# Macaron block on one core: expert rows stored raw with their mean and root, and a new order of the work ahead of the second router

## The reference

```python
x = x + 0.5 * ffn(layernorm(x))
x = x + mamba(layernorm(x))
x = x + 0.5 * ffn(layernorm(x))
```

## Time and profile before

| | us |
|---|---|
| median of 3 runs | 460.59 (459.33 to 460.80) |
| profiled execution | 461.21 |
| its span | 459.4 |
| TensorE busy | 404.0 (88%) |
| VectorE busy | 307.4 (67%) |
| ScalarE busy | 240.0 (52%) |
| GpSimd busy | 277.8 (60%) |

### The profile page before, as it was taken

How to read it: one execution, slowest core, us unless ns; L and a number is a source line. 1 busy time by engine, 2 the same in 40 slices (tenths; PEclk the granted TensorE clock), 3 DMA queues, 4 the chain that set the end, 5 groups by cost and what they waited for, 6 DMA issues and landing times.

```text
span 459.4 us, 9998 instructions
## 1 busy us (share of the span) xinstructions
PE 404.0 (88%) x2636; PEld 316.4 (69%) x2637; DVE 307.4 (67%) x761; ACT 240.0 (52%) x575; POOL 277.8 (60%) x262
## 2 busy tenths in 40 slices
PE   8779999999995998989979889984799999999940
PEld 6359999999994343434335346671499999999930
DVE  4824555555554967999989999999455555555516
ACT  4535444444434656686765867434454444444404
POOL 2167777777433252688685787765377777776330
PEclk9769999999997799999979999987699999999985
DMA  7942111112103200000000000001111111112026
GB/s 262 374 158 82 49 50 45 45 44 44 31 21 93 93 0 0 2 0 1 0 0 0 0 1 0 1 1 53 57 53 44 47 44 51 45 44 37 22 55 227
DMA packets 11964, 25.03 MB, mean 54 GB/s; under 512 B 3485, under 2 KB 4260, under 8 KB 11936
## 3 DMA queue, kind: packets, MB, share of 16 engines
q1 hardware_dynamic: 6944, 15.38, 9.5%
q0 software_dynamic: 4992, 9.32, 7.4%
HBM read 17.34 MB, written 8.26 MB: 56 GB/s over the span
## 4 chain that ended last, share of the span: by engine, by line
PE 65%; DVE 13%; ACT 7%; DMA 5%; issue 4%; POOL 4%; SPq 0%; POOLq 0%; ACTq 0%; DVEq 0%
PE ps L835 30%; PE ps L860 15%; PE ps L970 7%; DVE ring_space L1344 3%; DMA ring_space<-expert_rows 2%; ACT shared L705 2%; DVE stats L1097 2%; PE ps L830 2%; ACT ps L697 2%; POOL shared L486 2%; PE ps L957 2%; PE ps L951 2%; PE ps L903 1%; DMA xg<-xn_rows,get_i 1%; POOL rstd L398 1%
## 5 line engine op out<-in xcount | busy, mean ns | idle before, releaser
L835 PE MATMUL ps<-xT,w_now 128*128 128x128 f32 x1248 | 154.1, 277 | 0.8 <-ACT xT L574 0.7
L835 PEld LDWEIGHTS ps<-xT,w_now 128*128 128x128 f32 x1248 | 147.3, 194 | 1.4 <-ACT xT L574 1.1
L1226 DVE TENSOR_TENSOR hidden<-ps,hidden 128x256 f32<-128x256 f32 x156 | 58.9, 419 | 94.6 <-PE ps L835 94.6
L591 ACT ACTIVATE hidden<-ps 128x256 f32<-128x256 f32 x156 | 51.4, 381 | 111.2 <-PE ps L835 111.1
L434 POOL DMA_INDIRECT expert_rows<-ysb,put_i x78 | 79.9, 1024 | 46.5 <-DVE ysb L1234 30.1
L426 POOL DMA_INDIRECT xg<-xn_rows,get_i x78 | 80.6, 1034 | 45.1 <-issue 21.2
L486 POOL TENSOR_TENSOR shared<-ring_space,shared 128x512 f32<-128x512 f32 x64 | 81.9, 1287 | 35.5 <-DVE ring_space L1344 29.6
L860 PE MATMUL ps<-w_down,hidden 128*128 x624 | 82.1, 275 | 0.0
L970 PE MATMUL ps<-shared,consts 128*128 128x512 f32 x128 | 71.7, 644 | 7.6 <-POOL shared L486 7.4
L860 PEld LDWEIGHTS ps<-w_down,hidden 128*128 128x128 f32 x624 | 75.7, 192 | 0.2
L705 ACT COPY shared<-ps 128x512 f32<-128x512 f32 x64 | 37.6, 587 | 35.5 <-DVE ring_space L1344 18.2
(11 more groups left out here) (161 smaller groups left out, 410.6 us busy)
## 6 DMA issues: line engine op xcount, KB each, us to landing
w_gate_up<-in_experts SPq DMA_DIRECT2D x8, 512.0 KB, 8.6
xn_rows<-xn SPq DMA_DIRECT2D x8, 256.0 KB, 4.0
w_down<-in_experts SPq DMA_DIRECT2D x1, 2048.0 KB, 11.9
ring_space<-expert_rows SPq DMA_DIRECT2D x4, 512.0 KB, 5.9
xg<-xn_rows,get_i POOLq DMA_INDIRECT x78, 2.6
expert_rows<-ysb,put_i POOLq DMA_INDIRECT x78, 2.3
x<-in_x_rows SPq DMA_DIRECT2D x4, 256.0 KB, 4.5
ring_space<-expert_rows SPq DMA_DIRECT2D x4, 256.0 KB, 3.5
```

The lines of the kernel that those rows point to most:

```text
L591: nc.scalar.activation(gelu[:, slot % 2, half], ps[:, GATE_BANK[slot % 2], half], ACT.Gelu).then_inc(gelu_done, 1)
L835: m = pe.matmul(ps[:, bank, f * P:(f + 1) * P], w_now[:, slot % W_SLOTS, first + f * P:first + (f + 1) * P], xT[:, slot % X_SLOTS, :], sta ...
L1226: dve.tensor_tensor(hact[:, slot % H_SLOTS, half], ps[:, UP_BANK[slot % 2], half], gelu[:, slot % 2, half], ALU.mult).then_inc(hact_done, 1)
```

## The change

- `x` gets two more columns per row (130 words): the negated mean and the root. Rows go to DRAM as they are with these two (`x_rows` instead of `xn_rows`), and ScalarE's normalising ahead of both passes goes, with GpSimd's shift. VectorE normalises each gathered tile into one of 3 buffers `xh` (`normal_rows`), three tiles ahead; the turn reads `xh` and waits for it, and a gather waits for `rows_normal`.
- `centred_gate` and `out_gate` get a ninth column, -1/128, so that the product for the logits also gives the negated mean of the output; with the old rows' mean it gives the mean of the new rows (`new_mean`). The variance of the new rows is a Square with summed output on ScalarE (`square_rows`); GpSimd makes the root (`second_row_rstd`). `output_statistics` on VectorE goes.
- The root of y's variance is made on ScalarE by Ln and Exp (`y_rstd`) instead of GpSimd.
- TensorE's tail order: `y_rows(2)` and `through_w_out(0)` stand in front of the last `sum_states`, `through_w_out(1)` next, all `through_out_gate` before the last two `through_w_out`, then `prefix(1)`. 18 products of `keep_clock` become 6. Banks are moved so that this is free of conflicts.
- The down weights are loaded in three parts: 4 experts behind the stores, 2 behind the first gather, 2 behind the third.
- `ldiff` is made after the indices and expert numbers. The last additions write to `xn`, from which the output is stored.

The diff, cut:

```diff
-Y_BANK = (0, 1, 0, 6)
+Y_BANK = (0, 1, 3, 6)
+OUT_BANK = (2, 0, 4, 5)
+ONEHOT_BANK = 3
...
-SPARE_BANK = 0
+SPARE_BANK = 6
 PREFIX_BANK = 1
 B_LAG, C_LAG = 5, 4
+DOWN_PARTS = (None, 0, 4), (0, 4, 6), (2, 6, 8)
...
-        shift = sb("shift", [P, C])
-        neg_mean = sb("neg_mean", [P, C])
+        log_y = sb("log_y", [P, C])
+        old_mean = sb("old_mean", [P, C])
+        new_mean = sb("new_mean", [P, C])
+        row_var = sb("row_var", [P, C])
+        row_var_e = sb("row_var_e", [P, C])
+        row_mean, row_rstd = x[:, :, D], x[:, :, D + 1]
 
 
...
                 sp.dma_start(w_gate_up[:, e, :], experts_in[:, e, 0:GU]).then_inc(w_loaded, 16)
 
             for l in range(2):
-                rows = xn_dram[l].rearrange("(p c) d -> p c d", p=P)
+                rows = x_dram[l].rearrange("(p c) d -> p c d", p=P)
                 y_rows = y_dram[l].rearrange("(p c k) d -> p c k d", k=TOPK, p=P)
                 for g in range(GROUPS):
 
-                    wait_normalised(sp, 2 * l, g)
-                    sp.dma_start(rows[:, grp(g), :], xn[:, grp(g), :]).then_inc(xn_stored[g], 16)
+                    sp.wait_ge(row_rstd_ready, l * GROUPS + g + 1)
+                    if l:
+                        sp.wait_ge(row_mean_ready, 2)
+                    sp.dma_start(rows[:, grp(g), :], x[:, grp(g), :]).then_inc(x_stored[g], 16)
                 if l == 0:
-                    sp.dma_start(w_down[:], experts_in[:, :, GU:WCOLS]).then_inc(down_loaded, 16)
+                    for after, first, last in DOWN_PARTS:
+                        if after is not None:
+                            sp.wait_ge(gathered[after], 16)
+                        sp.dma_start(w_down[:, first:last], experts_in[:, first:last, GU:WCOLS]).then_inc(down_loaded, 16)
...
 
                 v = slice(g * GC, (g + groups) * GC)
-                pool.wait_ge(var_ready, s * GROUPS + g + groups)
-                pool.tensor_tensor(rstd[:, v], var_e[:, v], neg_half[:, v], ALU.pow).then_inc(rstd_ready, groups)
-
-            def mean_shift(s, g, groups=1):
-
-                v = slice(g * GC, (g + groups) * GC)
-                pool.wait_ge(rstd_ready, s * GROUPS + g + groups)
-                pool.tensor_tensor(shift[:, v], neg_mean[:, v], rstd[:, v], ALU.mult).then_inc(shift_ready, groups)
-
-            def rsqrt_y(g):
+                pool.wait_ge(var_ready, g + groups)
+                pool.tensor_tensor(row_rstd[:, v], var_e[:, v], neg_half[:, v], ALU.pow).then_inc(row_rstd_ready, groups)
+
+            def second_row_rstd(g):
+
                 v = grp(g)
-                pool.wait_ge(yvar_ready, g + 1)
-                pool.tensor_tensor(yrstd[:, v], var_y[:, v], neg_half[:, v], ALU.pow).then_inc(yrstd_ready, 1)
+                pool.wait_ge(row_squared, g + 1)
+                pool.tensor_scalar(row_var_e[:, v], row_var[:, v], 1.0 / D, EPS, ALU.mult, ALU.add).then_inc(row_var_made, 1)
+                pool.wait_ge(row_var_made, g + 1)
+                pool.tensor_tensor(row_rstd[:, v], row_var_e[:, v], neg_half[:, v], ALU.pow).then_inc(row_rstd_ready, 1)
 
             def add_output(q):
 
                 pool.wait_ge(out_scaled_s, q + 1)
-                pool.tensor_tensor(x[:, grp(q), :].rearrange("p c d -> p (c d)"),
-                                   x[:, grp(q), :].rearrange("p c d -> p (c d)"), out_scaled[:, q],
+                pool.tensor_tensor(rows_of(q), rows_of(q), out_scaled[:, q].rearrange("p (c d) -> p c d", c=GC),
                                    ALU.add).then_inc(out_added, 1)
 
             def ffn(l):
...
                     r = t % RING
                     if t >= RING:
-                        pool.wait_ge(x_turned, t0 + t - RING + 1)
+                        pool.wait_ge(rows_normal, t0 + t - RING + 1)
                     pool.indirect_dma_start(
-                        out=xg[:, r, :], out_offset=None, in_=xn_dram[l],
+                        out=xg[:, r, :], out_offset=None, in_=x_dram[l],
                         in_offset=bass.IndirectOffsetOnAxis(ap=get_i[:, t:t + 1].bitcast(U32), axis=0),
                         bounds_check=T - 1, oob_is_err=False).then_inc(gathered[r], 16)
...
-            def normalise(s, g):
-
-                act.wait_ge(shift_ready, (GROUPS if s else 0) + g + 1)
-                if s:
-                    act.wait_ge(xn_stored[g], 16)
-                for c in range(g * GC, (g + 1) * GC):
-                    i = nc.scalar.activation(xn[:, c, :], x[:, c, :], ACT.Identity, bias=shift[:, c:c + 1],
-                                             scale=rstd[:, c:c + 1])
-                i.then_inc(xn_ready, 1)
+            def y_rstd(q):
+
+                act.wait_ge(yvar_ready, q + 1)
+                nc.scalar.activation(log_y[:, grp(q)], var_y[:, grp(q)], ACT.Ln).then_inc(log_y_made, 1)
+                act.wait_ge(log_y_made, q + 1)
+                nc.scalar.activation(yrstd[:, grp(q)], log_y[:, grp(q)], ACT.Exp, scale=-0.5).then_inc(yrstd_ready, 1)
 
             def scale_output(q):
 
                 act.wait_ge(yrstd_ready, q + 1)
                 act.wait_ge(out_done, q + 1)
                 for c in range(GC):
-                    i = nc.scalar.activation(out_scaled[:, q, c * P:(c + 1) * P], ps[:, 2 + q, c * P:(c + 1) * P],
+                    i = nc.scalar.activation(out_scaled[:, q, c * P:(c + 1) * P], ps[:, OUT_BANK[q], c * P:(c + 1) * P],
                                              ACT.Copy, scale=yrstd[:, q * GC + c:q * GC + c + 1])
                 i.then_inc(out_scaled_s, 1)
+
+            def square_rows(q):
+
+                act.wait_ge(out_added, q + 1)
+                act.wait_ge(row_mean_ready, 1)
+                for c in range(GC):
+                    at = q * GC + c
+                    i = nc.scalar.activation(out_scaled[:, q, c * P:(c + 1) * P], x[:, at, 0:D], ACT.Square,
+                                             bias=new_mean[:, at:at + 1], accum_out=row_var[:, at:at + 1])
+                i.then_inc(row_squared, 1)
 
...
-            for g in range(GROUPS):
-                scale_output(g)
-            for g in range(GROUPS):
-                normalise(2, g)
+            y_rstd(0)
+            scale_output(0)
+            y_rstd(1)
+            scale_output(1)
+            y_rstd(2)
+            y_rstd(3)
+            scale_output(2)
+            scale_output(3)
+            for q in range(GROUPS):
+                square_rows(q)
             row_ids(1)
             second_weight(1)
             ffn(1)
...
 
-                def turn_x(t, slot, n):
-                    r = slot % RING
-                    pe.wait_ge(gathered[r], (l * PER_SLOT[r] + n + 1) * 16)
+                def turn_x(t, slot):
+                    pe.wait_ge(rows_normal, t0 + t + 1)
                     if past(t0 + t - 1):
...
                         y_rows(0)
                         y_rows(1)
                         through_out_gate(0)
+                    if n == N - 1:
+                        pe.wait_ge(c_copied, GROUPS * N)
+                        y_rows(2)
+                        through_w_out(0)
                     sum_states(GROUPS - 1, n, False)
                     if n + B_LAG < N:
                         spread_b(GROUPS - 1, n + B_LAG)
                     if n + C_LAG < N:
                         spread_c(GROUPS - 1, n + C_LAG)
                 pe.wait_ge(yvar_ready, 1)
-                y_rows(2)
-                through_out_gate(1)
+                through_w_out(1)
                 y_rows(GROUPS - 1)
-                through_out_gate(2)
-                through_out_gate(GROUPS - 1)
-                pe.wait_ge(c_copied, GROUPS * N)
+                for q in range(1, GROUPS):
+                    through_out_gate(q)
                 pe.wait_ge(h_ready, GROUPS * N)
-                for q in range(GROUPS):
+                for q in range(2, GROUPS):
                     through_w_out(q)
+                prefix(1)
                 pe.wait_ge(yvar_ready, GROUPS)
-                keep_clock(8)
+                keep_clock(6)
 
...
             onehot(0)
             ffn(0)
             mamba()
-            prefix(1)
-            keep_clock(10)
...
                 dve.tensor_tensor(ldiff_raw[:], best[:, 1], best[:, 0], ALU.subtract)
-                if l:
-                    output_statistics(0)
-                    output_statistics(1)
-
                 dve.wait_ge(prefix_ready, l + 1)
...
-                if l:
-                    output_statistics(2)
-                    output_statistics(3)
-
...
-                dve.wait_ge(rstd_ready, (2 * l + 1) * GROUPS)
-                dve.tensor_tensor(ldiff[:], ldiff_raw[:], rstd[:], ALU.mult).then_inc(ldiff_ready, 1)
                 chain(dve.tensor_tensor(le_end[:], spread(consts[:, K_TILE:K_TILE + NT], 2, [P, NT, E]),
...
                 dve.tensor_scalar(get_i[:], put_i[:], 1, T - 1, ALU.logical_shift_right, ALU.bitwise_and).then_inc(index_ready, 1)
```

(27 more changed lines are left out.)

149 lines of the change are left out of this document (74 added, 75 removed).

## The result

| 20 runs of each | median us | lowest to highest |
|---|---|---|
| before | 459.88 | 456.76 to 461.07 |
| after | 461.95 | 459.28 to 464.77 |

The ratio after/before is 1.0058 [1.0035, 1.0082], so the change costs 0.6% (2.7 us by the ratio, 2.1 between the medians). The forecast was 4.7 us faster, with a chance of 0.11 on slower.

The account below looks back on a forecast made before the run. TensorE's two expert passes, 39 tiles each, were taken to bound the kernel, with gains only from its waits between them: -1.0 + 0.4 - 4.1 = -4.7, so 456.5 us against 461.21; range 452.4 to 459.9.

Parts of the forecast that it names:

- The steady step: Expert loop: normal_rows adds 0.34 us on VectorE per step, hidden under TensorE's gate and up products, so costs nothing.
- The rival on the slower side: Expert loop: normal_rows in front of the turn comes late, 0.22 us in each of 76 steps, 473 us; chance 0.11.
- C: Rival theory of the experiments, expert loop: VectorE copies lengthened by GpSimd's gathers are the whole loss; no chance given.
- A: Theory of the experiments, expert loop: TensorE's sequencer, held at the turn's wait, needs about 1.5 us to the next gate load.
- Start of the first pass: First gather to first turn: gather 2.76 instead of 4.19 us, normal_rows with semaphore adds 0.4; 1.0 us gained.
- Middle: Four statistics groups, on the path to each root: one more 4-column product each; 0.4 us lost, between 0 and 0.7.
- Tail: Mamba part's end up to the routing: TensorE work put ahead makes deviation start at 304.0 instead of 301.77, 2.3 later.
- The picks: Second routing on VectorE: two GpSimd additions beside them cost 1.6 us; picks end at 311.8, 1.1 later than before.
- The squares: ScalarE ahead of the row ids: 16 squares at 0.61 us each, 9.8 in all, leaving ScalarE free at 317.6.
- Second start: Start of the second expert pass: indices at 322.0 instead of 327.13, first turn at 326.7 instead of 330.80, 4.1 us gained.
- The milder rivals: Tail's gain given back by TensorE's lower clock and squares of 0.7, 458.9, chance 0.17; late w_down, 458.4, chance 0.08.
- w_down arriving late: First pass: the last 0.5 MB of down weights could come 2 to 3 us late, 458.4 us; chance 0.08.

Follow-up runs that it names:

- e2: The changed kernel with TensorE's register load of the next tile's expert moved ahead of the turn's wait: 454.36 us, ratio to before 0.9902.
- e5: The changed kernel with the normalising instruction issued twice per tile, first into a buffer nobody reads: 468.55 us, ratio to before 1.0204.
- e10: The kernel before plus one VectorE multiply by one per tile, directly behind h_act, which the turn waits for: 460.68 us, ratio 1.0024.
- e4: The kernel before plus one VectorE multiply by one per tile, last in the step, which the turn waits for: 467.67 us, ratio 1.0196.
- e3: The changed kernel with normal_rows directly behind h_act, ahead of the copies of the result and up weights: 453.38 us, ratio to before 0.9884.
- e6: The changed kernel with normal_rows ahead of the copies and w_down loaded in one DMA again: 453.46 us, ratio to before 0.988.
- e7: The changed kernel with normal_rows ahead of the copies and TensorE's new tail order undone, all through_w_out last: 456.63 us, ratio to before 0.9962.

## Why the prediction was wrong, point by point

**The step that failed is "The steady step": "0.34 and some 0.1 for two semaphores leave about 0.3 us. So it costs nothing".** The price was right (342 ns), the deadline was not. I measured the slack up to the start of the turn. But the wait of the turn holds up TensorE's sequencer, and the gate load behind the turn is 1.00 after it in a full step while the sequencer needs about 1.51 from its release. So the wait must be over 0.51 ahead of the turn. With an undisturbed copy of 0.43 normal_rows mostly ends 0.39 to 0.52 ahead: the slack was nothing, not 0.3. Three things then push a step over: 0.11 where VectorE starts its step late (gate at turn + 1.12), a copy lengthened beside GpSimd (0.67: + 1.36), and the jump back (+ 1.37 to 1.60). 7.7 us in all, and by the excess of each step over half of it at the eight jumps back. In the kernel before the turn waited for the gather, which was long done, so the sequencer ran ahead and none of this had a price; that is why no row of before showed it.

The Trainium skill (Perfetto Trace Analysis, "Sequencer Loop") says that a sequencer reads an instruction and pushes it into the engine's queue, and that the instruction waits for its semaphores there. By that alone the instructions behind a late turn would be in the queue already when it starts. These traces don't agree for the turn on TensorE: in every steady step of after, e2 to e5 and e10 the sequencer's next instruction came 0.05 after the end of normal_rows, and in after, e4 and e5 the distance to the gate load was 1.48 to 1.54 in most late steps outside the jump back.

**The rival on the slower side** had the place right ("normal_rows in front of the turn") and the point from which it decides wrong: "when normal_rows takes 0.7 or more". It counted the same deadline. Its 473 assumed a copy that is blocked until the gather ends in every step. 22 of the 33 copies between 40 and 136 us took 0.43 in after, 11 took 0.50 to 0.68 (before: 31 of 34 took 0.43). Each of these 11 ends 0.22 to 0.23 after the end of the gather beside it. So the rule of the Trainium skill cited there (SBUF — State Buffer, "Who interferes with whom") again shows in part: no copy was blocked for the whole gather, but the collisions became more frequent, and with no slack left they could push a step over. C is a part of A's loss, not a rival: e3 has 18 copies over 0.5 in both passes and no long step.

**Start of the first pass**: 0.7 instead of 1.0 in this pair, and not for the reason I gave. From the issue to the end of normal_rows it took 28.68 - 25.51 = 3.2, with one load of w_down in e6 just as much, 28.56 - 25.32 = 3.2. Over all traces the first turn lies at 28.8, 28.8 and 29.5 with the old stores and load (e10, e4, before), and at 28.6 to 29.6 with the new ones, in e7 at 31.7. So no gain is shown there. The split that I counted on costs 1.2 us behind the first turn at the full clock (e6 above).

**Middle**: 0.0 in the table; the 0.4 lost did not show, and over the traces this stretch spreads from 46.6 to 48.4.

**Tail**: the time of deviation was right to 0.2 (304.0, measured 304.23), but by two errors that cancel: the tail grew by 1.5, not by 2.3, and the start of the scans was 3.3 later in this execution with the scans 2.3 shorter.

**The picks**: raw_rows ended at 306.47 (forecast 306.3), picks at 311.6 (311.8). Two collisions with GpSimd's additions, 1.01 and 0.83 instead of 0.29, make 1.3 (forecast 1.6).

**The squares**: mis-sized. I took 0.61 each. The read of the sum is an instruction of its own, 0.21 as I guessed, but it overlaps the next square: they start 0.38 apart, 16 in 6.2 us, not 9.8. So in_tile (315.27, forecast 315.0) decides, as I had said for the lower end.

**Second start**: indices at 320.84 (forecast 322.0), up weights 324.30, first turn 325.37 (326.7). 5.4 earlier instead of 4.1. The forecast's own terms, 322.0 + 3.2 + 0.92 + 0.4, give 326.5 and not 326.7, which would have made it 4.3. Summed up, the parts outside the loop were forecast at -4.7; e3, which has all of them and no loop loss, measures 453.38 against 458.79, -5.4.

**The milder rivals**: TensorE's clock did go to its lower level. The windows view gives a granted clock of 1.00 up to 304 us, 0.82 for 304 to 306 and 0.50 (1.2 GHz) for 306 to 312. What TensorE did before the fall was the 24 router products of 9 columns each, from 301.45 to 304.19. In after it hit the end of the output products and the prefix (1.14 instead of 0.70), not the router products, which took 2.74 (forecast 3.1, the rival 4.6); in e7 they took 3.46. w_down arriving late did not happen: the down weight loads have 0.2 us of idle time in the whole span.

## What to carry to other kernels

A wait on TensorE had to be over well before its own instruction was due, and the same is worth asking of any engine: find the next instruction behind it that must not be late, and take the slack to that one, less the time that the queue needs to issue what stands between. Where the releasing engine has a free choice, make the releasing instruction first in its step; here one move of a call is worth 1.7%. And compare single profiled executions by section, with sections that the change doesn't touch as the control.
